# Routed rows returned by an indexed DMA instead of a one-hot matmul, gelu and one elu in two parts, and another order of the pieces on every engine

## The reference

```
x = x + L0_gnn(layernorm(x), adj)     # mlp 256->512, attention over 512 features, mlp 512->256, masked attention
x = x + L0_ffn(layernorm(x))          # routed feed-forward, below
x = x + L1_gnn(layernorm(x), adj)     # masked attention
x = x + L1_ffn(layernorm(x))          # mamba2: conv of 4 taps, scan, 8 heads, gate, rms norm, two matrices
```

```
weights = x @ wr + br                              # 256 weights, one a row
_, idx = top_k(weights, 128); sel_idx = idx[:127]  # 127 of the 256 rows are taken
sel = x[sel_idx]
h = gelu(sel @ w1 + b1)                            # 127 x 1024, tanh form
y = (h @ w2 + b2) * weights[sel_idx]
return zeros_like(x).at[sel_idx].set(y) + x        # rows that were not taken get 0
```

## Time and profile before

| | us |
|---|---|
| median of 3 runs | 3693.15 |
| the profiled execution | 3692.62 |
| its span | 3690.9 |
| PE busy | 3571.9 (97%) |
| DVE busy | 2996.4 (81%) |
| ACT busy | 2398.3 (65%) |
| POOL busy | 1181.0 (32%) |

### The profile page before, as it was taken

One profiled execution on the slowest core, in us unless ns is written; L12 is line 12 of the kernel. 1 busy time (PEld: TensorE's weight loads), 2 busy tenths in 40 slices (PEclk: granted clock), 3 DMA queues, 4 the chain that ended last, 5 costly groups with the idle time before them and its releaser, 6 DMA issues.

```text
span 3690.9 us, 64095 instructions
## 1 busy us (share of the span) xinstructions
PE 3571.9 (97%) x20632; PEld 3118.1 (84%) x20632; DVE 2996.4 (81%) x7921; ACT 2398.3 (65%) x5442; POOL 1181.0 (32%) x1950
## 2 busy tenths in 40 slices
PE   5799999999999999999999999999999999999976
PEld 4688888888888888888888888888888888888864
DVE  3478888888888888888888888888888888888875
ACT  2357667666666666666666766766766766766754
POOL 0123333332332332332332332332332333333332
PEclk8899999999999999999999999999999999999997
DMA  3001111101111111111111111111111111111010
GB/s 106 21 32 39 48 34 39 48 34 39 48 34 39 48 34 39 48 34 39 48 34 39 48 35 40 46 41 35 44 48 34 40 48 34 39 48 34 33 41 32
DMA packets 89156, 152.04 MB, mean 41 GB/s; under 512 B 13088, under 2 KB 75424, under 8 KB 80928
## 3 DMA queue, kind: packets, MB, share of 16 engines
q1 hardware_dynamic: 78576, 134.79, 10.9%
q0 software_dynamic: 6176, 16.79, 1.3%
q10 hardware_dynamic: 4368, 0.03, 0.1%
HBM read 117.49 MB, written 34.08 MB: 41 GB/s over the span
## 4 chain that ended last, share of the span: by engine, by line
PE 94%; DVE 2%; ACT 1%; issue 1%; POOL 1%; DMA 0%; ACTq 0%; POOLq 0%; DVEq 0%
PE A L1274 12%; PE M L1410 7%; PE A L1311 6%; PE A L1263 6%; PE Q L1397 6%; PE A L1294 6%; PE M L1502 6%; PE Q L1390 6%; PE M L1444 6%; PE M L1487 5%; PE Q L1321 3%; PE A L1359 3%; PE A L1321 3%; PE Q L1359 3%; PE A L1304 2%; PE Q L1404 1%
## 5 line engine op out<-in xcount | busy, mean ns | idle before, releaser
L1274 PE MATMUL A<-w_fc,o1T 128*128 128x256 f32 (+1 forms) x2048 | 464.5, 380 | 2.0 <-ACT o1T L597 2.0
L1274 PEld LDWEIGHTS A<-w_fc,o1T 128*128 128x128 f32 x2048 | 378.4, 190 | 51.9 <-issue 1.4
L546 POOL TENSOR_TENSOR xdt<-xr,dt 128x1024 f32<-128x1024 f32 x64 | 126.9, 1983 | 853.4 <-ACT xr L755 853.4
L769 ACT ACTIVATE dec<-cumB,cumcol 128x256 f32<-128x256 f32 (+1 forms) x1024 | 379.1, 443 | 1.1 <-DMA cumB<-cum_dram 1.1
L1089 DVE SCALAR_TENSOR_TENSOR acc<-M,w_conv,acc 128x255 f32<-128x255 f32 (+2 forms) x768 | 315.1, 469 | 4.4 <-ACT acc L714 4.2
L552 POOL TENSOR_TENSOR rms<-ms,power 128x2 f32<-128x2 f32 x64 | 44.5, 696 | 831.6 <-DVE ms L1172 831.6
L1410 PE MATMUL M<-xT_m,w_in 128*128 128x256 f32 x1280 | 287.0, 379 | 0.5 <-DVE tz L1136 0.5
L1146 DVE TENSOR_TENSOR dec<-dec,cb 128x1024 f32<-128x1024 f32 (+1 forms) x256 | 245.1, 957 | 41.4 <-ACT dec L773 34.8
L1410 PEld LDWEIGHTS M<-xT_m,w_in 128*128 128x128 f32 x1280 | 243.0, 190 | 33.9 <-DVE tz L1136 0.9
L597 ACT ACTIVATE o1T<-A,c_mlp 128x256 f32<-128x256 f32 x256 | 107.6, 471 | 236.0 <-PE A L1263 236.0
L695 ACT ACTIVATE wcol<-wsum,c_route 128x2 f32<-128x2 f32 x64 | 18.9, 296 | 366.7 <-PE Q L1242 366.7
(11 more groups left out here) (238 smaller groups left out, 9045.0 us busy)
## 6 DMA issues: line engine op xcount, KB each, us to landing
cumB<-cum_dram SPq DMA_DIRECT2D x64, 1024.0 KB, 4.7
x_in<-in_x SPq DMA_DIRECT2D x64, 256.0 KB, 4.8
x<-in_x SPq DMA_DIRECT2D x64, 256.0 KB, 2.8
out<-x3b SPq DMA_DIRECT2D x64, 256.0 KB, 2.2
sel<-sel_dram SPq DMA_DIRECT2D x64, 128.0 KB, 2.2
sel_dram<-xn_q,place POOLq DMA_INDIRECT x128, 2.4
w_mlp<-in_L_gnn_mlp_w SPq DMA_DIRECT2D x2, 512.0 KB, 6.2
w_fc<-in_L_gnn_W_fc SPq DMA_DIRECT2D x2, 512.0 KB, 8.5
```

The source lines that it names most:

```text
L769: last = nc.scalar.activation(dec[:, h, :], columns[:, h, :], ACT.Relu, bias=cumcol[:, side, h:h + 1], scale=-1.0)
L1274: last = nc.tensor.matmul(rows1(half, u, 2), o1T[:, k, u * P:(u + 1) * P], w_fc[:, k, half, 0:D + 2 * i], start=(k == 0), stop=(k == KH - 1))
```

## The change

Three things are changed.

**Routing.** `pick`, `pickT`, the two transposes, the copy and the `q_scatter` matmuls are gone. In their place SyncE's new `q_keep` stores `yff` in rows 0 to 127 of a second DRAM scratch, `yff_dram`, whose other rows are zeroed once, and GpSimd's new `q_fetch` gathers from it by two indirect DMAs with the same `slot` numbers (the former `place`) that sent the rows away, into `yback`. `q_x2` waits for that and reads `yback` from SBUF.

**Parts.** Each of the gelu's five steps is done in two halves of 512 columns, with a semaphore count for each, and `q_ffn2.0` on TensorE needs the first half only. `a_att`, `a_elu_b`, `a_elu_c` and `a_uturn` go by the two halves of the features.

**Order.** Every list in `STEPS` is new. On TensorE the lags still run to 5; on VectorE they run from 0 to 7 (before 0 to 6).

```diff
 STEPS = {
     "tensor": [
-        ("m_da", 5), ("a_mlp1.0", 1), ("a_mlp1.1", 1), ("q_ffn1.1", 3), ("a_fc.0", 1), ("m_cum_col", 5),
...
+        ("a_fc.0", 1), ("a_fc.1", 1), ("q_gather", 3), ("a_bcast", 1), ("q_ffn1.0", 3), ("q_ffn1.1", 3),
...
     "sync": [
-        ("m_store", 7), ("q_sel", 4), ("a_residual", 3), ("m_spread", 6), ("a_load", 0),
+        ("a_load", 0), ("m_spread", 6), ("q_sel", 4), ("m_store", 7), ("q_keep", 4), ("a_residual", 1),
...
+            def q_keep(b):
+
+                if not (isinstance(b, int) and b < 2):
+                    sp.wait_ge(yff_back, 32 * (b - 1))
+                    sp.nop(nofuse=True)
+                sp.wait_ge(S["yff_ready"], b)
+                sp.dma_start(yff_dram[0:P, :], yff[:]).then_inc(yff_sent, 16)
...
+            def q_fetch(b):
+                before(pool, S["x2_ready"], b)
+                after(yff_sent, 16 * b)
+                pool.nop(nofuse=True)
+                for u in range(U):
+                    nc.gpsimd.indirect_dma_start(yback[:, u, :], None, yff_dram,
+                                                 bass.IndirectOffsetOnAxis(slot[:, u:u + 1], 0)).then_inc(yff_back, 16)
...
-            def a_elu_b(b):
-
-                act.wait_ge(S["e1_ready"], b)
-                nc.scalar.activation(e1m[:], e1[:], ACT.Relu, bias=1.0, scale=-1.0).then_inc(S["e1m_ready"], 1)
-                act.wait_ge(S["e1m_ready"], b)
-                nc.scalar.activation(e1x[:], e1m[:], ACT.Exp, scale=-1.0).then_inc(S["e1x_ready"], 1)
+            def a_elu_b(b, half):
+
+                cols = slice(half * D, (half + 1) * D)
+                act.wait_ge(S["e1_ready"], nth(b, 2, half + 1))
+                nc.scalar.activation(e1m[:, :, cols], e1[:, :, cols], ACT.Relu, bias=1.0, scale=-1.0)\
+                    .then_inc(S["e1m_ready"], 1)
...
             def q_gather(b):
                 act.wait_ge(S["sel_ps"], b)
-                nc.scalar.copy(pickT[:], Q0[:, 0:N])
                 nc.scalar.copy(selT[:], Q0[:, N:].rearrange("p (k r) -> p k r", k=KD)).then_inc(S["sel_ready"], 1)
...
-                for u in range(U):
-                    last = nc.vector.tensor_scalar(pick[:, u, :], slot[:], rank[:, u:u + 1], None, ALU.is_equal)
-                last.then_inc(S["pick_ready"], 1)
...
             def q_x2(b):
-                v.wait_ge(S["sc_ps"], b)
+                v.wait_ge(yff_back, 32 * b)
...
-                    last = nc.vector.scalar_tensor_tensor(out=x2[:, u, :], in0=two(Q1)[:, u, :], scalar=wcol[:, u:u + 1],
+                    last = nc.vector.scalar_tensor_tensor(out=x2[:, u, :], in0=yback[:, u, :], scalar=wcol[:, u:u + 1],
...
             def q_ffn2(b, i):
-                pe.wait_ge(S["gl_ready"], b)
+                pe.wait_ge(S["gl_ready"], nth(b, 2, i + 1))
...
-            def q_scatter(b):
-                pe.wait_ge(S["yff_ready"], b)
-                for u in range(U):
-                    last = nc.tensor.matmul(Q1[:, u * D:(u + 1) * D], pickT[:, u * P:(u + 1) * P], yff[:],
-                                            start=True, stop=True)
-                last.then_inc(S["sc_ps"], 1)
```

More of the change, by code:

```diff
@@ L37 @@
-        ("g_att", 3), ("b_res", 1), ("b_pturn", 1), ("q_gather", 2), ("a_turn", 0), ("b_att", 1), ("m_xbc_a", 4),
-        ("m_xbc_b", 4), ("q_ffn1.0", 2),
[3 rows of a table added]
+        ("b_proj", 1), ("m_z.0", 4), ("m_out.0", 5), ("b_bcast", 1), ("m_out.1", 5), ("m_ss", 5), ("a_turn", 0),
+        ("g_turn", 3), ("m_dt", 4), ("g_proj", 3), ("b_pturn", 1), ("m_z.1", 4), ("g_bcast", 3), ("b_att", 1),
+        ("q_route", 2), ("m_xbc_a", 4), ("b_res", 1), ("m_xbc_b", 4), ("m_da", 4), ("a_mlp1.0", 0), ("m_cum_col", 4),
@@ L39 @@
+        ("g_pturn", 3), ("a_mlp1.1", 0), ("g_att", 3),
     ],
     "vector": [
[L41 to L48, removed]
+        ("m_out", 7), ("m_dt", 6), ("g_proj", 5), ("q_route", 4), ("b_pturn", 3), ("g_mask", 5), ("m_gate", 6),
@@ L49 @@
+        ("g_lrelu", 5), ("g_max", 5), ("q_rank", 4), ("b_elu_c", 3), ("b_x1", 3), ("g_pturn", 5), ("m_scan", 6),
+        ("m_conv_b.0", 6), ("m_conv_b.1", 6), ("m_cum_col", 6), ("m_conv_b.2", 6), ("a_fc", 2), ("g_elu_b", 5),
+        ("m_silu", 6), ("g_x3", 5), ("a_fcol", 2), ("m_silu_bc", 6), ("a_maxima", 2), ("m_stats", 5),
[4 rows of a table added]
+        ("m_sq", 6), ("b_mask", 2), ("g_norm", 4), ("b_lrelu", 2), ("m_ms", 6), ("b_max", 2), ("a_norm", 0),
+        ("q_norm", 3),
     ],
     "scalar": [
-        ("q_route", 2), ("a_mlp2", 1), ("g_exp", 3), ("b_proj", 1), ("m_dt_exp", 4), ("g_pturn", 3), ("m_z", 4),
@@ L52 @@
[L52 to L55, removed]
+        ("m_xbc_b", 5), ("g_pturn", 4), ("a_mlp1", 1), ("g_elu", 4), ("g_att", 4), ("m_silu", 5), ("m_decay.0", 5),
[3 rows of a table added]
@@ L56 @@
+        ("b_proj", 1), ("g_turn", 3), ("b_exp", 1), ("m_dt_exp", 4), ("g_proj", 3), ("b_pturn", 1), ("m_z", 4),
+        ("a_turn", 0), ("b_att", 1), ("q_route", 2), ("b_elu_b", 1), ("g_exp", 3), ("m_xbc_a", 4),
     ],
     "gpsimd": [
-        ("q_norm", 3), ("m_xrow", 6), ("g_norm", 4), ("m_rms", 6), ("q_send", 3), ("m_dt_log.0", 5), ("m_turn", 5),
-        ("a_norm", 0), ("m_dt_log.1", 5), ("q_turn", 3), ("m_da", 5), ("m_norm", 4),
+        ("g_norm", 5), ("m_rms", 7), ("q_turn", 4), ("m_dt_log.0", 6), ("m_dt_log.1", 6), ("m_da", 6), ("q_send", 4),
@@ L199, in gnn_ffn_mamba_kernel @@
         rank = sb("rank", [P, U])
-        pick = sb("pick", [P, U, P])
-        place = sb("place", [P, U], U32)
+        slot = sb("slot", [P, U], U32)
         sel = sb("sel", [P, D])
-        pickT = sb("pickT", [P, N])
+        yback = sb("yback", [P, U, D])
         selT = sb("selT", [P, KD, P])
@@ L488, in q_send @@
             def q_send(b):
-                after(S["place_ready"], b)
+                ready(S["slot_ready"], b)
                 before(pool, S["sel_ps"], b)
@@ L526, in m_dt_log @@
                 assert len(links) == CHAIN
-                for i in ((0, 1), range(2, CHAIN))[half]:
+                for i in ((0, 1, 2, 3, 4, 5), range(6, CHAIN))[half]:
                     if i:
@@ L1198, in _ @@
                 **parts("m_mix", m_mix, 4), **parts("m_y", m_y, 2), m_dt=m_dt, m_sq=m_sq, m_ms=m_ms, m_out=m_out),
-                dict(a_fc=fc_columns, a_elu_c=masks, b_proj=gat_columns, b_mask=combined))
+                {"a_fc": fc_columns, "a_elu_c.0": masks, "b_proj": gat_columns, "b_mask": combined})
         @block.tensor
@@ L1373, in q_gather @@
             def q_gather(b):
-                pe.wait_ge(S["pick_ready"], b)
-                for u in range(U):
-                    nc.tensor.transpose(Q0[:, u * P:(u + 1) * P], pick[:, u, :], ident[:])
                 pe.wait_ge(sel_back, 16 * b)
```

148 lines of the change are left out of this document (78 added, 70 removed), and 9 rows, old and new, of the table STEPS.

## The result

The changed kernel takes 3806.91 us (median of 4 runs, 3803.88 to 3810.16), the kernel before 3693.37 us on the same chip (4 runs, 3691.35 to 3693.95). The ratio is 1.0309, with a 95% interval of 1.0296 to 1.0322: 3.1% slower. The forecast was 3653 us, with a range of 3612 to 3704. It was wrong in its sign, and the result lies outside the range.

The account below looks back on a forecast made before the run. PE was taken to bound the kernel at 55.02 us a turn; 53.93 + 0.2 + 0.1 gave 54.2, -48 us over 59 turns, +8 for filling and draining: 3651 us span, 3653 us forecast, range 3612 to 3704.

Parts of the forecast that it names:

- Off PE: On PE, dropping the `pickT` product (0.87 us) and the `pick` transposes (0.22) leaves 53.93 us a turn without waits.
- Place (2): From `a_att.0` to `a_mlp2.0`, hand-overs between PE, DVE and ACT: 0.1 us of wait a turn, ends 0 and 0.5.
- My walk: Following the new turn through from `a_fc.0` on PE, timing who waits for whom; it found four places.
- Place (1): At `a_bcast`, PE waits for DVE's copy of `f`, covered only by the `sel` transposes: 0.2 us a turn.
- Place (3): At `m_da`, PE's 15.1 us of own work covers the 14.5 us `dt` chain: wait 0, far end 0.4.
- Place (4): `yff` returned by store and gather before `q_x2` on DVE: hidden with 1.5 us to spare, wait 0.
- Ends: Filling and draining outside the steady turns: +8 us in all, between -5 and +25.
- The loop does not close: Rival: loop from `a_bcast` over DVE, ACT, POOL to `m_da` and back takes 0.5 us more; 3682 us, chance 0.15.
- the fetch comes late: Rival: returned rows reach `q_x2` on DVE 2.0 us late, turn 56.2, 3771 us; chance 0.12.

Follow-up runs that it names:

- e8: e4 with the rows returned by the one-hot matmul again (`pick`, its transposes, `pickT`, `q_scatter`), without `q_keep` and `q_fetch`: 3722.87 us.
- e4: e3 with the transposes of `xr` (`m_xrow`) moved ahead of `a_bcast` on TensorE: 3658.95 us.
- e2: The changed kernel with one more wait on GpSimd, so `xdt` starts only after the first two products with `dec` on DVE: 3712.26 us.
- e3: The changed kernel with the output store moved behind `q_keep` on SyncE (lag 6), plus the later `xdt` of e2: 3663.12 us.
- e5: e3 with `xdt` released after the first product with `dec` instead of the second: 3731.73 us.
- e7: e4 with the gelu's four SBUF steps whole again, each at the place of its second half: 3894.15 us.

## Why the prediction was wrong

The steps by their numbers in the prediction:

- **Off PE, 1.09 us a turn.** Right: 1.08 (e8 against e4). But the 53.93 us that it left for a turn without waits took every other piece of PE as long as before, and that was too little: e4, where no wait shows, has 54.29.
- **Place (2), attention and gelu in halves.** This step failed, and it is the larger. It had 0.1 us, with 0.5 as the far end; it measured 1.64, and e2 gives 1.6 back. My walk had durations of DVE from an order in which `xdt` ran beside a PSUM step and batch statistics. In the kernel before POOL's `xdt` starts at 2009.30, beside the second residual that reads `Q` from PSUM, and takes 1.99:

```profile
2009.30 1.99 POOL L546 TENSOR_TENSOR xdt<-xr,dt 128x1024 f32<-128x1024 f32 x1 [13.35 <-ACT xr L755]
```

  I followed `xdt` only as load on POOL, not as something that stands beside DVE's steps. The walk was right that each piece comes 0.0 to 0.5 us ahead of need; so nothing was left to bear 1.7 us.
- **Place (1), `a_bcast`.** This step failed too. 0.2 taken, 1.05 measured, 0.26 where the store was moved (e3). The cover from PE was counted rightly; what was not followed is the chain into DVE from the other side: SP's place for the store, `x3b`, third residual, copy of `f`. On SP the store now stands behind the 1 MB load, and I had not followed it past that.
- **Place (3), `m_da`.** Right. POOL's `dt` chain from 2037.48 to 2045.59 is 8.1 us (8.4 said), and PE takes L1466 with no wait.
- **Place (4), the way of `yff`.** Right. `yff` is ready at 2018.90, the second gather is issued at 2022.93 and lands 3.0 later: 7.0 us, where I had 6.9. DVE takes `q_x2` at 2027.71 without a wait, 1.8 us later (1.5 said), and waits 1.10 us behind it at `b_mask`, for `b_bcast`, as foretold.
- **Ends.** +8 said, +12 measured in the changed kernel; in the profiled execution of e3 3666.5 - 59 x 54.39 = 457.5 us, +13.

With the two causes taken out the kernel is near the forecast, with a turn of 54.39 for 54.2 and 3663 us for 3653. The error is 59 x (1.64 - 0.1 + 1.05 - 0.2) = 141 us of the 154. Of the rest about 8 are PE's own work (54.07 without the two gaps, 53.93 said, over 59 turns) and about 4 the ends.

The Trainium skill ("SBUF — State Buffer", section "SBUF: two separate sides") says of VectorE and GpSimd that they share a port pair as an exclusive lock, held for a whole instruction, and counts a VectorE step with two SBUF inputs beside a GpSimd step that reads SBUF among the cases. The prediction had this rule in hand and weighed it at one place, the indirect DMAs of the fetch. There nobody waits for them: the two issues took 1.24 and 1.28 us in the changed kernel, beside products with `dec`, and 1.06 and 0.96 in e5. It asked the rule about the new instructions of the change. The instructions that collided were both old; only their neighbours were new. The large steps here agree with the rule: 0.68 to 2.36 us on DVE, 1.27 to 1.86 and 2.20 on POOL. One pair does not, a power step of POOL (last section).

Of the rivals none was this one. "The loop does not close" and "the fetch comes late" both sought a wait in the new transfers and the known chains. That a reordered kernel may change durations, and not only the order, had no case and no chance of its own.

## What to carry to other kernels

When a change reorders DVE and POOL, write down for each large POOL tensor operation which DVE instructions now stand beside it, and add the full remaining time of the one to the other wherever the DVE instruction has two inputs in SBUF; durations from the old trace hold only for the old neighbours. Release such a POOL operation by a step of DVE behind which a PSUM-reading step follows: one semaphore wait was worth 1.6 us a turn here. And follow a moved store backwards from its buffer: who refills it, and who waits for that.

## What the runs showed of the hardware

- A DVE step with two inputs in SBUF and a large tensor operation of POOL (128x512 or 128x1024) did not share time here: the second to start waited for the end of the first. The held DVE step (the gelu's cube step and the product with `dec`) ended 0.55 us after `xdt` in both kernels, and `x3b` 1.13 us after DVE's step in two of two. `u` with one operand in PSUM took 0.87 us beside `xdt`, its usual time.
- This does not hold for every POOL operation. Its power step on 128x16 takes 3.03 us, and a DVE step with two inputs in SBUF (`xn_q` and `w_route`) that starts inside it takes 0.43 us; its median over the 64 turns is 0.43 as well, against 0.42 in the kernel before, where POOL is idle beside it. The same instruction took 1.48 us once, while the pipeline fills (at 117.89), where `xs`, 128x512, stood beside it. Whether the small size or the kind of operation decides was not tested.

```profile
2037.78 3.03 POOL L532 TENSOR_TENSOR dt_w<-dt_w,inverse 128x16 f32<-128x16 f32 x1
...
2037.97 0.43 DVE L1047 SCALAR_TENSOR_TENSOR wrow<-xn_q,w_route 128x256 f32<-128x256 f32 x1
```

- A 256 KB store issued 1.1 us behind a 1 MB load on the same queue landed after 5.3 us, and after 2.2 away from it. A gather of 128 rows of 1 KB from DRAM landed after 3.0 us, its issue took 1.24 to 1.28 in the changed kernel.
- With a wait of 2.21 us in each turn (e7) TensorE's granted clock was 0.62 in the 4 us behind it at 2056.50, and `q_ffn2` took 5.1 to 5.3 us in 50 of 58 turns; in the other 8 it took 3.55 after the same wait. With 1.47 us a turn it took 3.57. So the length of the wait alone does not decide it, and what does stays open.
- Open too: why the new order has 0.35 us more in the turn than the old one at the same routing (e8, 55.37 against 55.02). The rows show where: from one start to the next the first attention, `q_ffn2`, the transposes of `u`, `q_scatter` and the product with `w_hand` each take about 0.1 us more in e8 (0.51 in sum), and the transposes of `xn_g` and `b_att` 0.22 less.
